# Gathers of the last four token tiles wait for a counted number of stored blocks, and the weighted additions stand closer together

## What is computed

```python
x = x + xattn(layernorm(x), ctx, ctx, mask, ...)
xf = layernorm(x).reshape(4096, 256)
scores = sigmoid(xf @ gate_weight.T)                  # 32 experts
topk_idx = ...                                        # 6 experts of each token, out of 4 of 8 groups
tw = scores[topk_idx] / sum * 2.5
for e in range(32):
    o = (silu(xf @ gu[e][:128].T) * (xf @ gu[e][128:].T)) @ dn[e].T     # 128 wide inside
    routed += combine[:, e] * o
x = x + routed + shared_expert(xf)
```

## Time and profile before

| what | before |
|---|---|
| median of three runs | 813.57 us (811.62 to 813.82) |
| span of the profiled execution, first to last instruction | 809.6 us |
| expert phase, first to last `hidden` (L1438) | 422.2 to 782.8 us |
| gathers (L546), first and last start | 484.9 and 801.1 us |
| last addition starts | 803.97 us |
| PE busy, share of the span | 91% |
| DVE, ACT, POOL busy | 64%, 48%, 66% |
| DMA engines' busy share, 485 to 700 us | 0.85 |

### The profile page before, as it was taken

One profiled execution on the slowest core, in us unless ns is written; L12 is line 12 of the kernel. 1 busy time (PEld: TensorE's weight loads), 2 busy tenths in 40 slices (PEclk: granted clock), 3 DMA queues, 4 the chain that ended last, 5 costly groups with the idle time before them and its releaser, 6 DMA issues.

```text
span 809.6 us, 18582 instructions
## 1 busy us (share of the span) xinstructions
PE 734.4 (91%) x5770; PEld 650.9 (80%) x5770; DVE 518.8 (64%) x1619; ACT 389.1 (48%) x832; POOL 536.7 (66%) x794
## 2 busy tenths in 40 slices
PE   6899999999999999986389999999989999899970
PEld 3788898889888888853169999899989999788860
DVE  5887777777777777755145334666666686646673
ACT  2454544444444444420026666665555665556540
POOL 0116878788788778867400007688978888778875
PEclk9899999999999999877699999999999999999995
DMA  9223334433333322214566558798978899778872
GB/s 290 78 54 105 125 125 131 131 124 115 114 127 130 126 72 85 79 66 145 183 195 183 173 165 244 220 266 241 288 232 264 246 275 270 224 228 252 255 222 84
DMA packets 113919, 140.27 MB, mean 173 GB/s; under 512 B 17103, under 2 KB 100691, under 8 KB 113824
## 3 DMA queue, kind: packets, MB, share of 16 engines
q1 hardware_dynamic: 90568, 84.75, 34.0%
q0 software_dynamic: 18432, 50.36, 20.4%
q10 hardware_dynamic: 4824, 3.99, 1.5%
HBM read 75.98 MB, written 63.06 MB: 172 GB/s over the span
## 4 chain that ended last, share of the span: by engine, by line
PE 31%; POOL 30%; issue 20%; DVE 11%; another core or an unknown queue 3%; DMA 2%; SPq 1%; ACT 1%; DVEq 0%; POOLq 0%; ACTq 0%
POOL rows L509 19%; PE sc_ps L1007 16%; PE bank L1019 8%; POOL work L499 7%; PE sc_ps L991 4%; POOL rstd L519 2%; DVE work L1464 2%; DVE work L1483 2%; DVE firsts L1041 1%; DMA store<-in_x 1%; POOL work L546 1%; DMA work<-tabd 1%; DVE work L1438 1%; DVE work L1157 1%
## 5 line engine op out<-in xcount | busy, mean ns | idle before, releaser
L1007 PE MATMUL sc_ps<-work 128*128 128x128 f32 x1792 | 221.0, 277 | 4.4 <-issue 1.8
L1007 PEld LDWEIGHTS sc_ps<-work 128*128 128x128 f32 x1792 | 210.3, 193 | 6.9 <-issue 4.5
L546 POOL DMA_INDIRECT work<-yrows,dest x192 | 188.5, 982 | 36.1 <-POOL work L499 20.5
L509 POOL DMA_INDIRECT rows<-work,dest x192 | 187.7, 977 | 35.0 <-issue 34.8
L499 POOL MEMSET work<- 128x304 f32 (+1 forms) x366 | 137.3, 375 | 104.7 <-DMA yrows<-work 88.9
L1438 DVE TENSOR_TENSOR work<-work,sc_ps 128x256 f32<-128x256 f32 x112 | 46.9, 419 | 128.9 <-issue 72.5
L1019 PE MATMUL bank<-wdn,work 128*128 x448 | 116.7, 383 | 9.9 <-issue 5.3
L1019 PEld LDWEIGHTS bank<-wdn,work 128*128 128x128 f32 x448 | 76.5, 191 | 18.2 <-issue 12.3
L688 ACT ACTIVATE work<-bank 128x512 f32<-128x512 f32 x112 | 66.8, 597 | 40.6 <-PE bank L1019 22.5
L1464 DVE SCALAR_TENSOR_TENSOR work<-work 128x256 f32<-128x256 f32 x160 | 76.8, 480 | 10.8 <-DMA work<-yrows,dest 7.5
L596 ACT ACTIVATE work<-work 128x1232 f32<-128x1232 f32 x32 | 39.4, 1231 | 91.9 <-DVE work L1157 75.3
(11 more groups left out here) (168 smaller groups left out, 1105.0 us busy)
## 6 DMA issues: line engine op xcount, KB each, us to landing
work<-rows SPq DMA_DIRECT2D x224, 128.0 KB
yrows<-work SPq DMA_DIRECT2D x224, 128.0 KB
wgu<-in_egu SPq DMA_DIRECT2D x16, 512.0 KB
store<-in_x SPq DMA_DIRECT2D x8, 512.0 KB, 10.6
wdn<-in_edn SPq DMA_DIRECT2D x8, 512.0 KB
out<-work SPq DMA_DIRECT2D x32, 128.0 KB
rows<-work,dest POOLq DMA_INDIRECT x192
work<-yrows,dest POOLq DMA_INDIRECT x192
```

Source lines behind the costliest of these rows:

```text
L509: pool.indirect_dma_start(rows[:, :], bass.IndirectOffsetOnAxis(ap=dest[:, t, k:k + 1], axis=0), rowb[:, m, :], None).then_inc(scat[m], 16)
L546: pool.indirect_dma_start(yg[:, g % RG, :], None, yrows[0:n * P, :], bass.IndirectOffsetOnAxis(ap=dest[:, t, k:k + 1], axis=0)).then_inc(l ...
L1007: last = mm(ps8[2 + m % 2][:, (2 * w + g) * P:(2 * w + g + 1) * P], wst[w][m % 2][:, k * 2 * I + g * I:k * 2 * I + (g + 1) * I], xeT[:, m ...
```

## The change

- The additions are spread by another rule: addition g stands in step 26 + 15g // 32 (`ADD_AT`), so 32 additions take 15 steps where they took 16. The last stands in step 115. SP's `st_out` follows each tile's last addition by two steps (`OUT_AT`).
- Tiles 28 to 31 (KNOWN = 28) no longer wait for the largest possible block. One more matmul (`begun_ps`) sums `begun` over the experts for the last four tiles, DVE rounds each sum up to a multiple of 8 blocks and turns it into a semaphore value in the table (three `table` increments instead of two), and POOL loads that value into a register before the tile's first gather and waits for it on all eight `y_st`.
- Tiles up to 27 keep their rule, but the spread waits stop at the largest possible block of tile 27: gather 162 waits for block 198, and gathers 163 to 167 wait for no further one.
- SP writes zeros over blocks 184 to 223 of `yrows` in ten DMAs of 512 KB during tiles 22 to 31, since a gather may now be issued before the last blocks are stored.

```diff
-OUT0 = ADD0 + 3
+KNOWN = NT - 4
+FILL = 184
@@ build
+        begun_ps = bank[3][0:1, P + NTB:P + NTB + NT - KNOWN]
...
+        ADD_AT = [ADD0 + (g * 15) // 32 for g in range(NT * TOPK)]
+        OUT_AT = [ADD_AT[(t + 1) * TOPK - 1] + 2 for t in range(NT)]
+
+        def load_known(t):
+            _, got = nc.values_load_multi_w_load_instructions(
+                table[0:1, NTB + t - KNOWN:NTB + t - KNOWN + 1], engines=(mybir.EngineType.Pool,), min_val=16,
+                max_val=16 * NTB // RY)
+            return got[0]
@@ SP, ld_experts
+                f0 = FILL + 4 * (t - NT) + NTB - FILL
+                if f0 >= FILL:
+                    sp.dma_start(yrows[f0 * P:(f0 + 4) * P, :].rearrange("(j p) d -> p j d", p=P),
+                                 padrow[:, :].unsqueeze(1).broadcast_to([P, 4, D])).then_inc(tails_st[0], 16)
@@ SP
-                sp.wait_ge(tails_st[q], 16 * ((5, 6, 22)[q]))
+                sp.wait_ge(tails_st[q], 16 * ((5 + (NTB - FILL) // 4, 6, 22)[q]))
...
-            for n in range(OUT0 + NT * TOPK // 2):
+            for n in range(OUT_AT[NT - 1] + 1):
...
-                t, part = divmod(n - OUT0, TOPK // 2)
-                if part == TOPK // 2 - 1 and t >= 0:
-                    st_out(t)
+                for t in range(NT):
+                    if OUT_AT[t] == n:
+                        st_out(t)
@@ POOL, gather
-                need(pool, "dest2", t)
+                if t >= KNOWN:
+                    stored_by = load_known(t)
+                    need(pool, "dest2", t)
+                    for one in y_st:
+                        pool.wait_ge(one, stored_by)
+                else:
+                    need(pool, "dest2", t)
                 for k in range(TOPK):
                     g = t * TOPK + k
-                    if g == 0:
+                    if t >= KNOWN:
+                        pass
+                    elif g == 0:
...
-                    elif n - 1 + k < NTB:
+                    elif n - 1 + k < stored_before(KNOWN - 1):
@@ PE, number_blocks
+                mm(begun_ps, const("ones")[0:E, 0:1], begun[0:E, KNOWN + 1:NT + 1], start=True, stop=True)
@@ DVE, read_table
+                known = slice(NTB, NTB + NT - KNOWN)
+                ts(codes[:, known], begun_ps, float(RY - 1), None, ALU.add).then_inc(S_["sch"], 1)
+                v.wait_ge(S_["sch"], 17)
+                ts(table[:, known], codes[:, known], 3, 4, ALU.logical_shift_right,
+                   ALU.logical_shift_left).then_inc(S_["table"], 1)
@@ DVE, combine
-                for g in (2 * (n - ADD0), 2 * (n - ADD0) + 1):
-                    t, k = divmod(g, TOPK)
-                    if 0 <= t < NT:
+                for g in range(NT * TOPK):
+                    if ADD_AT[g] == n:
+                        t, k = divmod(g, TOPK)
...
-            for n in range(NPR + 2, ADD0 + NT * TOPK // 2):
+            for n in range(NPR + 2, ADD_AT[-1] + 1):
```

More of the change, by code:

```diff
@@ L549, in _ @@
             need(pool, "base", SB - 1 - SE, 2)
+            pool.wait_ge(S_["table"], 3)
             for t in range(NT):
```

## The result

The changed kernel takes 821.4 us (median of four runs, 817.69 to 824.55), where the kernel before has 813.6 on the same chip: a ratio of 1.0104, 95% interval 1.0071 to 1.0136. It is slower, by 7.8 us; 3.1 was forecast, with a range that reaches to 823.0. The profiled execution took 821.57 us with a span of 819.7, so 1.9 us lie around the span, where I had put 4.0. From trace to trace the last gather starts 9.9 us later (811.0, where it was 801.1), so more than the medians say.

A forecast was written before the change was run, and what follows sets the result against it. PE was taken to pace the expert phase and POOL's gathers the end. Gather 191 at 758.3 + 44.1 + 1.6 + 0.3 = 804.3 us, 3.1 us later, gave a span of 812.7 and a median of 816.7 us; range 809.5 to 823.0.

The forecast's parts named there:

- The bound: Expert phase paced by PE, 3.25 us a step on average; the end by POOL's gathers, 1.52 us each.
- the wait that does not end last: POOL's wait for the largest possible block, which the change shortens, ends 6.5 us before its gather; slots hold POOL instead.
- (a): Expert pipeline: distance from block to addition shrinks from 8 steps to 3, delaying pair 99's store 6.0 us (2.5 to 9.2).
- (b): POOL's run to the end: gather 191 starts 44.1 us after gather 162, before 46.25; a gain of 2.1 us.
- (c): Four register loads on POOL, 0.4 us each (0 to 1.4), so 1.6 us.
- (d): Ahead of the expert phase: one small matmul, two DVE operations and the table's loads, 0.3 us (0 to 0.6).
- (e): Ten stores of zeros, 5.2 MB, while the DMA engines are busy for 0.28: no cost.
- (f): `st_out` keeps its distance behind the additions, and DVE's 12 additions moved ahead of the last `hidden`: no effect.
- What was to show it: Signs: DVE waiting for gathers 10 us or more in steps 94 to 113, PE's end near 797 us, gathers at 1.5 us.
- The faster one: Rival: three steps of slack suffice in the pipeline and loads hide beside gathers; 4.6 us earlier, 809.0 us; chance 0.22.
- no change: Rival: the pipeline's delay is about as large as the gains, 3 to 5 us; chance 0.28.
- Transfers slower under load: Rival: store and gather transfers stretch under DMA load, delay 9.2 us, gather 191 7 us later, 820.6 us; chance 0.17.

The follow-up runs named there:

- Counted waits alone: The changed kernel with the additions back at their old places, two to a step: ratio 0.9994 to the kernel before.
- second group: Runs on one other chip: the changed kernel again (1.0185), additions two (0.9997) and four steps earlier (1.0158), and denser additions only from 162 on (0.9993).
- dense only behind 161: The changed kernel with two additions to a step up to 161 and five in two steps behind: ratio 0.9993 to the kernel before.
- `ADD0` = 24: The kernel before with every addition two steps earlier, still two to a step, 6 steps from block to addition: ratio 0.9997.
- third group: Runs on another chip: the kernel before again (1.0007) and three versions with counted waits for all tiles (1.0032, 0.9938, 1.0026).
- all counted, two steps earlier: The changed kernel with counted waits for all tiles, zeros over blocks 8 to 223 and every addition two steps earlier: 0.9938, 777.0 against 783.0 us.
- the two other versions with the same stores: The changed kernel with counted waits for all tiles and zeros over blocks 8 to 223: 1.0032 with its own additions, 1.0026 with the old ones.

## Why the prediction was right

**The bound and the wait that does not end last: right.** Counted waits alone moved nothing (0.9994). The evidence named for it was misread: the 36 waits for additions in rows 5 are 0.24 us each, and most of that is the pause of 0.16 us that every gather has. The slots do hold POOL on the first chip, but ahead of the memsets, for 15 us.

**(a), the delay by the shortened distance: right in kind, too small.** The step that failed is the size of the delay at the store of pair 99, 6.0 us between 2.5 and 9.2. Measured from the first `hidden`, that of pair 99 comes 12.5 us later than before (335.6 against 323.1 us). Half of that, 6.3 us, arises from step 72 on, where DVE waits for gathers. The other 6.2 us are there by step 72, where DVE had waited for one gather, for 1.0 us; the additions' waits don't explain them, and with one trace of each kernel they may be chance. In the second group, where the steps are quiet, it is plain: 325.3 us in the changed kernel, and 305.4 in the version that is dense only behind 161, whose additions stand as before up to there. That is 19.9 us, twice the upper bound. Missing from the sum were:

- The onset. But for addition 68, waits begin at addition 100, in step 72, where the distance is 5 and 4, and 15.5 of the 54.6 us lie before addition 130; in the second group it is 31.0 of 70.9. I had let steps up to 93 pass.
- POOL's rate inside the pipeline. I used 1.5 us for the run to the end and for the second block of a pair, but never held 2.13 gathers a step against it.
- The loaded transfers, a little. I allowed 0.8 us on 2.85 for gather to addition, so 3.65. Over the 46 additions inside the pipeline for which DVE waited, the median from the gather's start is 3.9 us. The Trainium skill, "DMA: Bandwidth & Descriptors", section "Latency and other measured facts", has the latency of HBM grow with its load; the trace agrees in direction, with 2.8 us at a DMA share of 0.44 and 3.9 at 0.75 to 0.82.

A fourth went the other way: DVE has idle time to spare in each step. The 47.6 us of waits at `ADD0` = 24 cost nothing, which the sum of (a) had no place for.

**(b), the run to the end: right.** 29 issues from gather 162 took 44.5 us (766.5 to 811.0); 44.1 and 1.6 for the loads were forecast, and 46.2 it was before.

**(c), the loads: too dear.** A load takes 0.52 us and 0.15 for the check [L369 above], but beside a gather: in three of the four tiles the gather behind the load follows the one ahead by 1.48 us as everywhere, in one by 1.67. So 0.05 us each, not 0.4.

**(d), (e), (f): right as far as one can tell.** The first `hidden` is 0.9 us later than before on the first chip, at 423.1; in the second and third group it lies between 405.8 and 410.0 with and without the change, once at 416.7 (all counted, two steps earlier). Whether the zero stores made that one late is open; the two other versions with the same stores have 408.4 and 409.4.

**What was to show it.** 8 additions behind the last `hidden`, DVE's waits over 10 us from step 94 to the last `hidden` (23.1), gathers at 1.5 us from 162 on: all there. The last `hidden` was to be near 795 us and is at 802.5. Gather 162 was to be at 758.3 and is at 766.5. One sign of being wrong is there in part, steps of 4 us and more from step 86: single steps reach 8.1 us, and the mean from there to the last is 3.72 us, where it was 3.28.

**The rivals.** The faster one fell with the waits of rows L1494, and no change with the interval of 1.0071 to 1.0136. Transfers slower under load, at 820.6 us, comes nearer to the 821.4 than the forecast's 816.7, and its 3.65 us from gather to addition nearer to the 3.9; but most of its missing delay is the onset and POOL's rate, which it hasn't either.

**What was luck.** In the traces the last gather is 9.9 us later, not 3.1; the median came 4.7 us above the forecast, and not 7, because the 4.0 us put on the span were 1.9 in the changed kernel. And the range reaches 1.2% above the kernel before. On the second group's chip the loss is 1.85% (1.37 to 2.33), which is outside it.

## What to carry to other kernels

Before work that waits for a transfer is moved closer to it, write down the distance in steps between the two and what must fit into it: here the chain of product, eviction, store, gather and addition was 11.5 us at gather 162, four steps are too few and six are enough. Then ask which engine ends last, and whether the new waits can reach what that engine waits for: 59 us of waits on DVE cost 0.3% where POOL waited for no late store, and 71 us cost 1.85% where it did. A wait that is put on a data-dependent count pays only where that wait ends last and whatever comes next (here ten slots and the place of the additions) is moved with it; the waits alone changed nothing, the denser additions alone cost 3%, both together with all tiles counted and an earlier start gained 0.6%. And hold every engine's rate per step against the step: an issuing engine at 1.48 us can't feed one that takes a row in 1.45. Last, read an engine's waits at the first instruction that stands behind them: here that is the memset, not the gather.

## What was unexpected of the hardware

In this kernel a pause between indirect DMAs is worth more than the issues that it costs. Without the memset ahead of each gather POOL's pitch fell from 1.48 to 1.25 us, and the kernel before became 6.7% slower, the changed one 2.9% slower than the kernel before where it had been 1.0 to 1.85%. Against the run with the waits alone, from 520 to 800 us, PE's gate-up products stand for 15.3 us where no wait of the profile ends the pause, instead of 2.9; from 500 to 800 us the granted clock is 0.93 instead of 1.00 and the DMA engines' share 0.69 instead of 0.81. The gathers come in bursts of six with long pauses between them. Why PE's issue slows beside them wasn't tried; it stays open.
